# Graph attention: one straight run of eight phases, the ramp in PSUM and the neighbour term added by GpSimd

## What is computed

```python
def gat_layer(x, adj, W, a_self, a_neigh, b):
    feat = jnp.einsum('nf,hfo->hno', x, W)
    attn_self = jnp.einsum('hno,ho->hn', feat, a_self)
    attn_neigh = jnp.einsum('hno,ho->hn', feat, a_neigh)
    e = attn_self[:, :, None] + attn_neigh[:, None, :]
    e = jax.nn.leaky_relu(e, 0.2)
    e = e + MASK_VAL * (1.0 - adj)[None, :, :]          # MASK_VAL = -1e10
    alpha = jax.nn.softmax(e, axis=-1)
    out = jnp.einsum('hnm,hmo->hno', alpha, feat) + b[:, None, :]
    out = jnp.transpose(out, (1, 0, 2)).reshape(out.shape[1], -1)
    return jax.nn.elu(out)

x = x + gat_layer(gat_layer(ctx, adj, W0, ...), adj, W1, ...)   # adj = layernorm(x)
```

## Time and profile before

| | |
|---|---|
| median of 3 runs | 2325.22 us |
| the profiled execution | 2323.65 us |
| its span (first to last instruction) | 2322.1 us |
| PE busy | 1861.5 us (80%) |
| DVE busy | 1542.1 us (66%) |
| ACT busy | 1108.2 us (48%) |
| POOL busy | 586.9 us (25%) |
| mean granted clock of TensorE | 0.897 |

### The profile page before, as it was taken

How to read it: one execution, slowest core, us unless ns; L and a number is a source line. 1 busy time by engine, 2 the same in 40 slices (tenths; PEclk the granted TensorE clock), 3 DMA queues, 4 the chain that set the end, 5 groups by cost and what they waited for, 6 DMA issues and landing times. The chain is left out here.

```text
span 2322.1 us, 35149 instructions
## 1 busy us (share of the span) xinstructions
PE 1861.5 (80%) x8271; PEld 904.7 (39%) x8272; DVE 1542.1 (66%) x3266; ACT 1108.2 (48%) x2014; POOL 586.9 (25%) x701
## 2 busy tenths in 40 slices
PE   1788866888745999999993288888889629999994
PEld 0444433344342555555551122222222414444442
DVE  5988877888766555565563377777776485555552
ACT  1988857888632232232232246666666522222221
POOL 3000012000101555455542211111111003444441
PEclk9799876999876999999996579999999859999997
DMA  4100122001172778889655831111111537988884
GB/s 131 47 37 39 32 79 83 38 1 60 37 230 75 173 174 228 220 182 224 119 100 158 171 57 52 51 51 51 51 51 35 187 104 181 229 230 226 229 213 110
DMA packets 201022, 275.48 MB, mean 119 GB/s; under 512 B 83372, under 2 KB 121740, under 8 KB 199820
## 3 DMA queue, kind: packets, MB, share of 16 engines
q1 hardware_dynamic: 158731, 173.28, 24.3%
q0 software_dynamic: 38544, 97.02, 21.0%
q10 hardware_dynamic: 3633, 3.88, 1.0%
HBM read 204.44 MB, written 73.37 MB: 120 GB/s over the span
## 5 line engine op out<-in xcount | busy, mean ns | idle before, releaser
L1876 DVE TENSOR_REDUCE a_negmax<-a_m 128x1 f32<-128x512 f32 x512 | 328.1, 686 | 101.7 <-PE a_m L1732 100.1
L1824 ACT ACTIVATE a_prob<-a_s 128x1024 f32<-128x1024 f32 x256 | 260.4, 1020 | 142.9 <-PE a_s L1743 137.4
L1268 PE MATMUL f_gu_bank<-f_wgu,f_xT 128*128 x768 | 269.4, 494 | 6.8 <-issue 4.1
L1732 PE MATMUL a_m<-a_kT,a_qT 112*128 (+1 forms) x512 | 198.5, 399 | 82.6 <-DVE a_negmax L1876 39.0
L354 PE MATMUL g_pt<-g_ident,g_p 128*128 128x128 f32 x1024 | 185.6, 311 | 95.6 <-ACT g_p L460 94.2
L1268 PE MATMUL s_gu_bank<-s_wgu,s_xT 128*128 128x512 f32 x512 | 232.0, 596 | 2.3 <-ACT s_xT L1320 1.6
L354 PEld LDWEIGHTS g_pt<-g_ident,g_p 128*128 128x128 f32 x1024 | 127.7, 156 | 239.0 <-issue 151.3
L460 ACT ACTIVATE g_p<-g_e,g_emin 128x512 f32<-128x512 f32 x256 | 184.2, 720 | 66.0 <-DVE g_emin L554 65.9
L1234 POOL DMA_INDIRECT tokens<-f_y,f_ids x96 | 152.1, 1584 | 222.5 <-DMA tokens<-f_y,f_ids 176.6
L544 DVE SCALAR_TENSOR_TENSOR g_l<-g_tb,g_s,g_h 128x512 f32<-128x512 f32 x256 | 190.4, 745 | 17.2 <-ACT g_h L438 17.2
L1268 PEld LDWEIGHTS f_gu_bank<-f_wgu,f_xT 128*128 128x128 f32 x768 | 143.3, 191 | 138.6 <-issue 60.9
(11 more groups left out here) (298 smaller groups left out, 2951.5 us busy)
## 6 DMA issues: line engine op xcount, KB each, us to landing
s_wgu<-in_L_ffn_w_gate_up SPq DMA_DIRECT2D x32, 1024.0 KB, 7.3
f_wgu<-in_L_ffn_gate_up_proj SPq DMA_DIRECT2D x32, 768.0 KB, 5.6
g_tb<-neighbours SPq DMA_DIRECT2D x8, 2048.0 KB
s_wd<-in_L_ffn_w_down SPq DMA_DIRECT2D x32, 512.0 KB, 4.1
a_qT<-q_parts SPq DMA_DIRECT2D x224, 64.0 KB, 2.2
f_wd<-in_L_ffn_down_proj SPq DMA_DIRECT2D x32, 384.0 KB, 5.8
q_parts<-p_part SPq DMA_DIRECT2D x48, 128.0 KB, 2.2
g_mask<-in_x SPq DMA_DIRECT2D x4, 1024.0 KB, 7.7
```

Of the source, the lines that this page charges most:

```text
L1268: last = nc.tensor.matmul(gu_bank[k % TR][:, 0:F], xT[k % TR][:, c, :], wgu[:, bass.ds(place, 1), c, :].rearrange("p a f -> p (a f)"), sta ...
L1732: nc.tensor.matmul(m_bank[n % RING][:, :], qT[k][0:PAIR_ROWS, head, st * P:(st + 1) * P], group_keys(G, PAIR_ROWS, slice(0, N)), start=Tru ...
L1824: nc.scalar.activation(prob[n % QR][:, :, :], s_bank[n % RING][:, :, :], ACT.Exp).then_inc(p_ready, 1)
L1876: V.tensor_reduce(negmax[k % RING][:, st, head:head + 1], m_bank[n % RING][:, :], X_AXIS, ALU.max, negate=True).then_inc(m_read, 1)
```

## The change

The two turns become one straight list of 256 units in eight phases. The order of the phases is that of before. Per unit:

- `relu` writes 4(t+s), ramped, into a PSUM bank (two banks `h_bank`, g_h), two units ahead (before: SBUF, four). It waits for `masked` of two units before.
- `low` is gone. In its place POOL adds the mask and the neighbour row: `near` = mask + t, in SBUF, four buffers (`add_neighbours`). The own term s falls out of the softmax there.
- `masked` (DVE) computes g_e = -near - h, one operand in SBUF and one in PSUM, with the minimum as before.
- DVE does all copies of `probT`, and in iteration n first the copy of unit n-2, then `masked` of unit n. There are two banks `pt_bank` instead of three.
- `z` and the exp of the elu are computed in place in the single `o_bank` (before: two banks, and two SBUF tiles). The matmuls into `o_bank` stand at j = 4 to 7 (before 3 to 6).

Around the units: the first batch's mask and the layer 0 terms are computed ahead of the units, the layer 1 vectors (`weigh`) in iterations 4 to 11, and each later mask in the phase ahead of its use: statistics, a square root on ACT, the normalisation on DVE at iterations 20 to 23, and `mask_tile` on POOL in the same iterations. The mask of the first batch is loaded from ACT's queue, all other loads from SP's in another order. `prepare` of the next layer 0 phase runs in the fourth phase.

```diff
@@ relu (ACT)
-                        act.wait_ge(low_ready, i * ALL_UNITS + (n + 1))
-                        nc.scalar.activation(high[:, n % LAG, :], t_all[k % SLOTS][:, h, :], ACT.Relu, scale=-4.0,
+                    if n >= H_BANKS:
+                        act.wait_ge(e_ready, n - H_BANKS + 1)
+                    nc.scalar.activation(h_bank[n % H_BANKS][:, :], t_all[k % SLOTS][:, h, :], ACT.Relu, scale=4.0,
@@ root (ACT), new; called at iteration 18 of the phase ahead
+                def root(m):
+                    act.wait_ge(var_done, m + 1)
+                    nc.scalar.activation(std[:, m, :], std[:, m, :], ACT.Sqrt).then_inc(std_done, 1)
@@ transposes (PE)
-                        pe.wait_ge(pt_act if on_act else pt_dve, i * (ACT_ALL if on_act else DVE_ALL) + (copies(on_act, before + 1) + AHEAD))
+                    if n >= PT_BANKS:
+                        pe.wait_ge(pt_ready, n - PT_BANKS + 1)
@@ masked (DVE)
-                        V.tensor_tensor_reduce(out=eneg[:, n % LAG, :], in0=lneg[:, n % LAG, :], in1=mask[k % SLOTS][:, local % NT, :],
-                                               scale=1.0, scalar=3.0e38, op0=ALU.add, op1=ALU.min,
+                    dve.wait_ge(high_ready, n + 1)
+                    dve.wait_ge(near_ready, n + 1)
+                    if n >= LAG:
+                        dve.wait_ge(p_ready, n - LAG + 1)
+                    V.tensor_tensor_reduce(out=eneg[:, n % LAG, :], in0=near[:, n % LAG, :], in1=h_bank[n % H_BANKS][:, :],
+                                           scale=-1.0, scalar=3.0e38, op0=ALU.add, op1=ALU.min,
@@ the list of DVE
-                    for n in range(LOW_AHEAD):
-                        low(n)
-                    for n in range(ALL_UNITS + 2 * PAIR):
-                        if n + LOW_AHEAD < ALL_UNITS:
-                            low(n + LOW_AHEAD)
-                        if n < ALL_UNITS:
-                            masked(n)
-                        if 2 <= n < ALL_UNITS + 2 and (n - 2) % PAIR not in ACT_COPIES:
-                            copy_probT(n - 2)
+                for n in range(ALL_UNITS + 2 * PAIR):
+                    if COPY_LAG <= n < ALL_UNITS + COPY_LAG:
+                        copy_probT(n - COPY_LAG)
+                    if n < ALL_UNITS:
+                        masked(n)
...
+                    if 4 <= n < 4 + 2 * FC:
+                        weigh(2 + (n - 4) // FC, (n - 4) % FC)
...
+                    for m in range(1, B):
+                        step = n - mask_phase(m) * UNITS - 16
+                        if step == 0:
+                            mask_statistics(m)
+                        if step == 1:
+                            mask_variance(m)
+                        if step == 3:
+                            mask_root(m)
+                        if 4 <= step < 4 + NT:
+                            mask_normal(m, step - 4)
@@ finish (DVE), the wait is on this pair's product as before
-                            V.tensor_tensor(z[:, :], o_bank[pr % RING][:, :], rall[:, :], ALU.mult).then_inc(z_ready, 1)
+                        dve.wait_ge(pv_done, pr + 1)
+                        V.tensor_tensor(o_bank[:, :], o_bank[:, :], rall[:, :], ALU.mult).then_inc(z_ready, 1)
@@ POOL
+                def mask_tile(m, t):
+                    tile = mask[m % SLOTS][:, t, :]
+                    pool.wait_ge(adj_ready, m * NT + t + 1)
+                    pool.tensor_scalar(tile, tile, -1.0, 1e10, ALU.add, ALU.mult).then_inc(mask_ready, 1)
...
+                    if n >= LAG:
+                        pool.wait_ge(e_ready, n - LAG + 1)
+                    pool.tensor_tensor(near[:, n % LAG, :], mask[slot][:, local % NT, :], t_all[k % SLOTS][:, local // NT, :], ALU.add).then_inc(near_ready, 1)
...
+                for n in range(ALL_UNITS + 3 * PAIR):
+                    if n < ALL_UNITS:
+                        add_neighbours(n)
+                    for m in range(1, B):
+                        t = n - mask_phase(m) * UNITS - 20
+                        if 0 <= t < NT:
+                            mask_tile(m, t)
@@ SP, one phase
+                def spread(k):
+                    sp.wait_ge(stT_ready, k + 1)
+                    sp.dma_start(t_dram.rearrange("(h n) -> h n", h=H), stT[k % SLOTS][H:2 * H, :]).then_inc(t_stored, 16)
+                    sp.wait_ge(t_stored, 16 * (k + 1))
...
+                    sp.dma_start(t_all[k % SLOTS][:, :, :].rearrange("p h n -> p (h n)"),
+                                 bass.AP(t_dram.tensor, t_dram.offset, [[0, P], [1, H * N]])).then_inc(t_in, 16)
```

More of the change, by code:

```diff
@@ L89, in graph_attention @@
     SLOTS = 2
[L90 to L91 removed]
+    PHASES = 2 * B
     UNITS = NT * H
@@ L96, in graph_attention, with phase, out_pair, mask_phase @@
     ALL_PAIRS = PHASES * PAIRS
-    OUT_PAIRS = SLOTS * PAIRS
-    ACT_COPIES = (0, 2, 4, 6)
-    RELU_AHEAD, LOW_AHEAD = 4, 2
+    OUT_PAIRS = B * PAIRS
+    H_BANKS, PT_BANKS = 2, 2
+    COPY_LAG = 2
     PREP_FIRST, PREP_FEAT = 10, 14
+    def phase(k):
+        half, rest = divmod(k, 2 * SLOTS)
+        layer, slot = divmod(rest, SLOTS)
+        return half * SLOTS + slot, layer, slot
+    def out_pair(pr):
+        half, rest = divmod(pr, 2 * SLOTS * PAIRS)
+        return half * SLOTS * PAIRS + rest - SLOTS * PAIRS
+    def mask_phase(m):
+        return m // SLOTS * 2 * SLOTS + m % SLOTS - 1
     with ExitStack() as stack:
@@ new lines, in _ @@
+                for t in range(NT):
+                    mask_tile(0, t)
+                for n in range(ALL_UNITS + 3 * PAIR):
[5 more added lines that the diff above has]
+                            mask_tile(m, t)
+                    if n == UNITS:
+                        for j in range(RING):
+                            load_old(j)
+                    pr, step = divmod(n - 3 * PAIR, PAIR)
+                    if 0 <= pr < ALL_PAIRS and phase(pr // PAIRS)[1] == 1:
+                        j = out_pair(pr)
+                        if step == 5:
+                            store_new(j)
+                        if step == 7 and j + RING < OUT_PAIRS:
+                            pool.wait_ge(xo_stored[j % RING], 16 * (j // RING + 1))
+                            load_old(j + RING)
@@ new lines, in _ @@
+                for n in range(PREP_FIRST, UNITS):
+                    prepare(0, n)
+                for n in range(ALL_UNITS):
+                    transposes(n)
+                    if n >= PAIR:
+                        finish(n // PAIR - 1, n % PAIR)
+                    if n >= 2 * PAIR:
+                        finish(n // PAIR - 2, n % PAIR + PAIR)
+                    if n // UNITS + 1 < PHASES:
+                        prepare(n // UNITS + 1, n % UNITS)
+                for step in range(PAIR):
+                    finish(ALL_PAIRS - 1, step)
+                    finish(ALL_PAIRS - 2, step + PAIR)
@@ new lines, in _, with prepare @@
+                act.dma_start(mask[0][:, :, :], rows_of(0)).then_inc(x_in[0], 16)
+                def prepare(k, n):
+                    batch, layer, slot = phase(k)
+                    if n == PREP_FIRST + 2 and layer == 0:
+                        act.wait_ge(xt_ps, batch + 1)
+                        nc.scalar.activation(xT0[slot][:, 0, :], prep_bank[1][:, :], ACT.Copy).then_inc(xt_ready, 1)
+                    t, rest = divmod(n - PREP_FEAT - NT, NT)
+                    if rest == 1 and 0 <= t < NT:
+                        act.wait_ge(feat_ps, k * NT + t + 1)
+                        nc.scalar.activation(feat[slot][:, t, :], prep_bank[(t + 1) % 2][:, :], ACT.Copy).then_inc(feat_ready, 1)
```

644 lines of the change are left out of this document (286 added, 358 removed).

## The result

The changed kernel takes **2366.68 us** in the median of 4 runs (2364.43 to 2369.97). The kernel before took 2325.51 beside it, so the ratio is 1.018, with a 95% interval of 1.016 to 1.020: slower by 41 us, where 23 were forecast. The profiled execution took 2364.43 us, its span is 2362.4.

A forecast was written before the change was run, and what follows sets the result against it. Before the change, DVE was taken to bound light stretches and PE those with preparation. From 2323.65, less 62.9 for start and turn boundary, plus 49.6 for the loop and 37 for masks, came 2347 us; 8-in-10 range 2290 to 2390.

The forecast's parts named there:

- So a light group takes 17.3 us: Eight units without layer 1 preparation: 17.3 us, 16.4 at full clock throughout, against 15.07 before.
- the ring: Every unit's loop of exp, transposes, copy, `masked` and relu: 3.51 us for two units, 14.1 for eight.
- the bubble at `z`: At j=0 `z` waits for the product with a copy queued behind: `masked` j=1 starts at 3.5 us instead of 1.8.
- Start and turn boundary: Unit 0 masked at 34.5 us, gaining 23.9; units 120 to 127 become an ordinary group of 17.6, gaining 39.0.
- 18.6 + 18.5: Units 0 to 15, two groups of eight with `weigh`: 18.6 us at slow clock, then 18.5 with no `z` yet.
- Preparation, 54.9 and 56.7: Units 40 to 63 take 54.9 us against 53.03 before; such stretches with layer 1 transposes take 56.7.
- Masks, 12.3 each: Three later masks, computed among the units: 12.3 us each, +37 in all (28 to 50 by the tile's ends).
- the lockstep: Mask iterations 20 to 23, where POOL and DVE wait for each other: 4.0 us per unit against 2.0, +7.9 per mask.
- rival (a): Elastic loop: waits fall into the ring's idle time, a light group takes 15.0 us, total 2286; chance 0.26.
- The drain behind a table load: Skill rule of about 1380 ns after each ACT table load: six loads add 8 us, 2355; left out of the sum.
- Rival (c): Port: DVE and POOL exclude one another, 0.6 us per unit in the ring, 154 us in all, total 2500; chance 0.04.
- Rival (d): Turns do not join because mask 2 is late for its statistics; 15 of the 39 us kept, total 2362; chance 0.04.

The follow-up runs named there:

- e1: Changed kernel with `masked` of unit n ahead of the copy of unit n-2: 2336.44 us, ratio 1.006.
- e2: Changed kernel with a copy lag of three units instead of two, the copy still ahead of `masked`: 2350.57 us, ratio 1.013.
- e3: Changed kernel with the product's matmuls one iteration earlier, at j = 3 to 6 as before the change: 2334.88 us, ratio 1.005.
- e7: Changed kernel with ACT's first feature copies ahead of the first ramps: 2362.23 us, ratio 1.016.
- e8: Changed kernel without the square root of the last three batches' variances and its six table loads: 2362.90 us, ratio 1.016.
- e5: Changed kernel with POOL's `mask_tile` six iterations later, at 26 to 29 instead of 20 to 23: 2355.70 us, ratio 1.013.
- e10: Changed kernel with `masked` first, product at j = 3 to 6, later mask tiles, weight products ahead of the units, features ahead of the ramps: 2282.10 us, ratio 0.982.
- e4: Changed kernel with the ramp in SBUF tiles instead of PSUM banks, so `masked` reads two SBUF operands: 2383.53 us, ratio 1.026.
- e9: Changed kernel with both `masked` ahead of the copy and the product at j = 3 to 6: 2320.56 us (10 runs), ratio 0.9985.

## Why the prediction was right, and where it was off

The direction held, and 2366.68 lies in the range; the forecast of 2347 was 20 us low: 15 in the units, 1.5 behind them, and some 3 in what lies around the span and between the profiled execution and the median. The 15 are what is left of 20 us that the terms were short and 4.7 that two of them, the start and the first mask, were long.

- **"So a light group takes 17.3 us"**: six such groups took 17.27 to 17.36, those of layer 1 phases 17.4 to 18.0 for 17.6, with the intervals as laid out (3.65 for 3.5, then 1.93, 1.64, 2.39 for 1.8, 1.8, 2.0, and 2.50 for 2.9 at the spread: the transposes ahead of it were at 1.2 GHz, 1.09 us, and those behind it at 2.4, 0.66, where the forecast had it the other way). e1 and e2 show the ring, e3 the bubble at `z`, each by a single edit. The relu into PSUM was 0.63 us for 0.60.
- **Start and turn boundary**: unit 0 at 31.92 for 34.5; the row's landing, at 30.49, was the last wait, 6.8 us after its issue at 23.71. Units 120 to 127 are an ordinary group, 18.41 us for 17.6. Of the 39 us 38.2 were gained, and of the start 26.5 where 23.9 were forecast.
- **"18.6 + 18.5" for the first 16 units**: the step that failed, 7 us short. The ring and `weigh` were priced well (units 4 to 11 took 21.4 us; eight times 2.0 and 0.7 is 21.6), though it is DVE and not the ring that sets the pace there: it is busy for 20.7 of the 21.4 us. What I left out is the filling of the ring: units 0 to 3 took 13.4 us, not 8. Exp 0 waited 4.0 us behind ACT's feature copies (e7) and 1.28 for its table. Units 12 to 15, where the first pair's spread and the next features' work fall, took 9.3 us instead of 8.
- **Preparation, 54.9 and 56.7**: 1.5 to 3.8 us short in each of four stretches, 10 us in all, the largest part that is left. The surplus is in the first of each three groups, 19.7 to 21.2 us where the forecast left some 18; the full groups took 18.8 to 19.2 for 19.1, the third, with six preparing iterations again, 18.7 to 19.1. The 54.9 is not the sum of the terms beside it: three groups of 19.1 less four matmuls of 0.9 are 53.7, so the terms were a further 1.2 us short in each stretch. In the longest, at 469.15 to 476.04, the spread at the low clock (1.98) is followed by a preparation matmul (1.89) and transposes (1.11) at that clock; I had priced the low clock for the light groups alone.
- **Masks, 12.3 each**: near in sum, in part by luck. Set against the intervals of a group without a mask, they cost 10.1, 12.0 and 11.4 us. A tile takes 0.62 us, the lower end, not 1.49, so the lockstep is 3.2 us instead of 4.0 and its four units cost 5.2 us in phase 1 where 7.9 were forecast. In phases 4 and 5 POOL's DMA issues (0.78 us each in the lockstep, which I had not counted) bring them back to 6.6 and 6.8. The statistics and the root cost 6.5 to 6.9 us for 6.0: the burst of statistics lies in the same queue place as the wait for `z` and adds to it (6.55 us). The lower end of the range was a slip: with tiles of 0.61 the terms give 26, as rival (a) has it, and not 28. The root's 2.9 us is there, but e8 shows that a part of it is hidden by what comes next.
- **The drain behind a table load**: a load takes 1.28 us and the instruction follows at once (408.79 to 410.09). The trace and e8 speak against the 1380 ns more that the Trainium skill gives ("ScalarE: Activation LUTs", section "What ACT_TABLE_LOAD costs").
- **Rival (a)**, an elastic loop: the trace denies it for this kernel, since light groups took 17.4 us and not 15. e1, e3 and e5 to e7 show what it lacked. That e10 comes to 2282, near its 2286, is a coincidence and no proof of it: e10 has five edits. Rival (c) is denied for `masked`, and holds for `weigh` (0.4 us on POOL), for e4, and for the first batch's normalisations, as the rival left open: beside POOL's tiles two of them took 0.84 us instead of 0.54 (21.45 and 22.21). Rival (d): no gap at the fourth phase.

Left open: why PE is granted the low clock for some 6 us in the light groups of e9 and some 3 in those of the change, with much the same idle time before (1.85 and 1.30 us against 2.83 and 1.31). The variants were not run with a spread of reciprocals that takes PE less time.

## What to carry to other kernels

A change that takes work off DVE and ACT, the two busiest of a light group, can still lose: count the cushions it spends. Here a buffer depth of four became two, a copy was put ahead of the instruction that frees that buffer, and a consumer was put one iteration behind its producer instead of two; each can be found beforehand by following one unit round the ring with start-to-start times. Then mend the widest wait first and price the small ones again: late tiles were worth 11 us with the narrow ring and about 23 once it was wide, early weights 1.6 and 12, while two large mends added to 46 us instead of 62, it seems because they shared TensorE's slack.

## What the runs showed of the hardware

- GpSimd's tensor_scalar on 128x512 fp32 by constants took 0.62 us with two operations (add -1, multiply by 1e10), while before, the single multiplication by 1e10 took 1.49; why is open. Its addition of two fp32 inputs takes 1.27 us.
- A DVE operation with two SBUF operands and a GpSimd addition exclude each other: 0.69 us became 1.38 when the addition started first (e9), and `masked` 4.07 when it started behind the second of four back to back (e4). With one operand in PSUM it kept to 0.67 to 0.69 us in all 256, 95 of them beside a GpSimd operation.
- A DVE tensor_scalar on one 128x512 fp32 tensor in SBUF with two per-partition scalars took 0.84 us beside GpSimd's tensor_scalar and 0.54 without it, and GpSimd's 0.83 instead of 0.62.
- ACT's relu from SBUF into PSUM is 689 ns long, into SBUF 722 (e4; 715 before), but from start to start both take 0.63 us (0.61 before).
- A table load took 1.28 us, and the next instruction of ACT started at its end (407.27 to 408.57, 408.79 to 410.09).
